# Graph-network layer in f32 on one core: the setup that builds the node table is reordered and its copies are shared between two engines

## What is computed

```python
h_s = s @ lin1_ws * a / 8                       # s: 64 scalars per node
h_v = einsum('nci,cd->ndi', v, lin1_wv) * a     # v: 32 vectors of 3
w   = silu(edge_scalars @ fc_w1) @ fc_w2        # 224 weights per edge
es, ev = h_s[edge_src], h_v[edge_src]           # gather of 160-float rows
# products of w, es, ev and edge_attr (e0, e1), summed over edge_dst
agg = segment_sum(products, edge_dst)
out = layernorm(x + gated(x @ sc + agg @ lin2))
```

## Time and profile before

| what | us |
| --- | --- |
| median of 3 runs, without profiler | 4014.98 |
| span of the profiled execution | 4805.3 |
| first gather of table rows begins (profiled) | 74.7 |
| last gather begins (profiled) | 4767.4 |

### The profile page before, as it was taken

How to read it: one execution, slowest core, us unless ns; L and a number is a source line. 1 busy time by engine, 2 the same in 40 slices (tenths; PEclk the granted TensorE clock), 3 DMA queues, 4 the chain that set the end, 5 groups by cost and what they waited for, 6 DMA issues and landing times.

```text
span 4805.3 us, 64016 instructions
## 1 busy us (share of the span) xinstructions
PE 3953.4 (82%) x18658; PEld 1603.5 (33%) x18658; DVE 2421.9 (50%) x7622; ACT 1987.8 (41%) x5178; POOL 2967.8 (62%) x3160
## 2 busy tenths in 40 slices
PE   8778888888888888888888888888888888888887
PEld 5233333333333333333333333333333333333333
DVE  5455545555454544555555445555545545454544
ACT  3344444444444444344444344444444434444444
POOL 3666666666666666666666666666666666666664
PEclk9999999999999999999999989999999999999999
DMA  6443434343434343334343334343434333333333
GB/s 216 146 106 102 106 102 106 102 107 102 108 99 108 102 106 97 105 102 106 103 107 101 104 99 105 102 106 103 107 103 106 102 105 103 105 103 104 103 103 87
DMA packets 366207, 515.47 MB, mean 107 GB/s; under 512 B 66498, under 2 KB 245578, under 8 KB 365486
## 3 DMA queue, kind: packets, MB, share of 16 engines
q0 software_dynamic: 150768, 256.60, 22.7%
q10 hardware_dynamic: 164378, 180.74, 12.1%
q1 hardware_dynamic: 50724, 74.13, 5.1%
HBM read 431.15 MB, written 80.06 MB: 106 GB/s over the span
## 4 chain that ended last, share of the span: by engine, by line
another core or an unknown queue 35%; ACT 21%; PE 20%; issue 14%; ACTq 8%; SPq 0%; DMA 0%; DVE 0%; DVEq 0%
ACT aggsb L759 13%; ACTq L778 6%; PE pst_e L1061 6%; PE psg L1074 5%; PE psg L1072 5%; ACT tsum L783 3%; PE psw L1053 3%; ACTq L766 2%; ACT L804 1%; ACT hid L749 1%; PE psx L1097 1%; PE psx L1045 1%; ACT vec_s L800 0%; ACT L749 0%
## 5 line engine op out<-in xcount | busy, mean ns | idle before, releaser
L710 POOL DMA_INDIRECT rows<-h_table,src_cols x3125 | 2953.5, 945 | 1799.9 <-issue 894.8
L557 DVE TENSOR_TENSOR prod<-psw,rows 128x384 f32<-128x384 f32 (+2 forms) x3128 | 1210.1, 449 | 1680.8 <-remote 1264.3
L1072 PE MATMUL psg<-tsum,shifts 128*64 128x320 f32 x3126 | 1101.8, 478 | 653.3 <-ACT tsum L783 462.6
L1053 PE MATMUL psw<-fc,hid 128*128 128x448 f32 x3128 | 1424.0, 579 | 7.7 <-issue 1.7
L759 ACT ACTIVATE aggsb<-psg 32x160 f32<-32x160 f32 x3128 | 917.0, 293 | 927.2 <-remote 744.2
L1074 PE MATMUL psg<-tsum,shifts 128*64 128x288 f32 x3126 | 1009.2, 449 | 0.0
L1053 PEld LDWEIGHTS psw<-fc,hid 128*128 128x128 f32 x3128 | 549.0, 196 | 949.6 <-issue 840.1
L1061 PE MATMUL pst_e<-prod,sel 128*32 128x448 f32 x6256 | 811.9, 593 | 2.4 <-issue 2.4
L1072 PEld LDWEIGHTS psg<-tsum,shifts 128*64 128x64 f32 x3126 | 385.9, 144 | 1122.2 <-ACT tsum L783 774.3
L783 ACT ACTIVATE tsum<-pst_e 128x448 f32<-128x448 f32 x782 | 424.8, 543 | 499.0 <-remote 369.4
L1045 PE MATMUL psx<-es,fc 128*128 128x512 f32 x782 | 415.7, 613 | 175.5 <-ACT turned L788 120.5
(11 more groups left out here) (151 smaller groups left out, 1511.2 us busy)
## 6 DMA issues: line engine op xcount, KB each, us to landing
es<-in_esP ACTq DMA_DIRECT2D x391, 256.0 KB
agg_table<-aggsb ACTq DMA_DIRECT2D x782, 80.0 KB
rows<-h_table,src_cols POOLq DMA_INDIRECT x3125
nag<-agg_table SPq DMA_DIRECT2D x96, 320.0 KB
nxin<-in_xN SPq DMA_DIRECT2D x96, 208.0 KB
h_table<-hrow ACTq DMA_DIRECT2D x24, 320.0 KB, 4.2
out<-yn SPq DMA_DIRECT2D x95, 80.0 KB
xa<-in_xaT SPq DMA_DIRECT2D x24, 256.0 KB, 4.0
```

The costliest lines, as they stand in the source:

```text
L557: return nc.vector.tensor_tensor(out, w_part, ev, ALU.mult)
L710: nc.gpsimd.indirect_dma_start(out=rows[:, u * QT + j, :], out_offset=None, in_=m.h, in_offset=bass.IndirectOffsetOnAxis(ap=m.src[:, t:t + ...
L1053: ins = nc.tensor.matmul(psw[b][:, 2 * c:2 * c + 2, 0:WN], hid[:, at:at + P], m.fc2[:].rearrange("p (t w) -> p t w", t=2)[:, :, 0:WN], sta ...
L1072: nc.tensor.matmul(psg[0:2 * W, 0:2 * AW].rearrange("p (s c) -> p s c", s=2), shifts[:, q % PRING, h, 0:2, :], low, start=(h == 0), stop=( ...
```

## The change

What it does, in the order of the work:

- SyncE loads chunks 0 to 3, then `m.dst` and `tbase`, then four new loads of `qbase` (each 32 partitions, a row of 782 int32 broadcast), and only then chunks 4 to 24. The loop over chunks is written out. The twelve `late` loads of fc1 and fc2 move from GpSimd's queue to the end of SyncE's. The load of the first 128 source columns moves from SyncE's end to the head of ScalarE's queue.
- Of each chunk ScalarE copies the first half (two groups, two instructions) and VectorE the second half (one `tensor_tensor` of 128x320). ScalarE issues the store of chunk n after its own copies of chunk n + 1.
- VectorE's other setup work is dealt out between its copies, unit by unit. Four pairs of 32-partition subtractions over `tbase` become two 128-partition ones with `qbase`; `after` is made from 780 columns in place of 3124 and its extreme is taken over these.
- `xa`, `xz` and `hrow` lie in the part of `m.e4` that is loaded later; `rows` and `prod` are allocated outside both blocks.
- SyncE waits for no store of the table. GpSimd waits for them at the head of the edge block, after its `value_load` and before its first gather; ScalarE waits for them before it loads the rest of `m.e4` in round 1.

TensorE's instructions per chunk stay the same.

```diff
         @block.sync
-            for c in range(1, SLOTS):
-                load_x(c, c, CB * P)
+            for c in range(1, 4):
+                load_x(c, CB * P)
             sp.dma_start(m.dst[:], io["dstT"]).then_inc(s_dst, 16)
             sp.dma_start(tbase[:], io["tile_base"].to_broadcast([P, TILES])).then_inc(s_dst, 16)
-            with sp.Fori(1, rounds) as i:
-                for c in range(SLOTS):
...
+            for j in range(QT):
+                sp.dma_start(qbase[W * j:W * j + W, :], io["quad_base"][j:j + 1, :].to_broadcast([W, QUADS])).then_inc(s_dst, 16)
+            for c in range(4, HCHUNKS):
+                load_x(c, CB * P)
+            load_x(HCHUNKS, rest)
             sp.dma_start(m.e4[:, 0:E4_FIRST, :], io["e4T"][:, 0:E4_FIRST, :]).then_inc(s_edge, 16)
-            sp.dma_start(m.src[:, 0:SRC_FIRST], io["srcT"][:, 0:SRC_FIRST]).then_inc(s_edge, 16)
-            for c in range(SLOTS):
-                sp.wait_ge(s_hout[c], 16 * (rounds + (2 if c == 0 else 0)))
-            sp.wait_ge(s_edge, 32)
+            sp.wait_ge(s_fc, 1)
+            sp.sem_inc(s_tick, 1)
+            for dst, src in late:
+                sp.dma_start(dst, src).then_inc(s_fcw, 16)
+            sp.wait_ge(s_edge, 16)
+            sp.wait_ge(s_fcw, n_fcw)
             sp.wait_ge(m.es_loaded, 16)
...
         @block.gpsimd
-            pool.wait_ge(s_fc, 1)
-            for dst, src in late:
-                pool.dma_start(dst, src).then_inc(s_w, 16)
-            pool.wait_ge(s_w, n_w)
+            pool.wait_ge(s_src, 16)
...
         @block.vector
+            def high_half(n, kind, c):
+                if kind == "h" and c >= SLOTS:
+                    dve.wait_ge(s_hout[c % SLOTS], 16 * (c // SLOTS))
+                    dve.sem_inc(s_tick, 1)
+                dve.wait_ge(s_high, second_halves(n) + 1)
+                out, scale = hrow[:, c % SLOTS, 2:CB, :], a_rows[:, CB * c + 2:CB * c + CB].unsqueeze(2)
+                nc.vector.tensor_tensor(out, psh[n % 2][:, 1, 0:2 * F].rearrange("p (b f) -> p b f", f=F),
+                                        scale.to_broadcast([P, 2, F]), ALU.mult).then_inc(s_highcp, 1)
...
+            for n, (kind, c) in enumerate(UNITS):
+                if n == 1:
+                    identity()
+                if n == 2:
+                    clear()
+                if n == 4:
+                    shift_pattern()
+                if n == 6:
+                    dve.wait_ge(s_dst, 32 + 16 * QT)
+                    then(local_nodes(0))
+                if n == 7:
+                    then(local_nodes(1))
+                if n == 8:
+                    window_starts()
+                if n == 9:
+                    window_steps()
+                if n == 10:
+                    reach()
+                if n == 11:
+                    extreme(0, m.local[:], ALU.max)
...
+                high_half(n, kind, c)
...
         @block.tensor
+            for n, (kind, c) in enumerate(UNITS):
                 keep_warm(256)
-                pe.wait_ge(s_xin[c], arrived)
+                pe.wait_ge(s_xin[c % SLOTS], 32 * (c // SLOTS + 1))
...
+                if n >= 2:
+                    pe.wait_ge(s_lowcp, n - 1)
...
+                    half(n, 0, [P, P], left, last).then_inc(s_low, 1)
+                    if n >= 2:
+                        pe.wait_ge(s_highcp, second_halves(n - 1))
+                    half(n, 1, [P, P], left, last).then_inc(s_high, 1)
...
         @block.scalar
+            act.dma_start(m.src[:, 0:SRC_FIRST], io["srcT"][:, 0:SRC_FIRST]).then_inc(s_src, 16)
...
+            for n, (kind, c) in enumerate(UNITS):
+                low_half(n, kind, c)
+                if n and UNITS[n - 1][0] == "h":
+                    store(UNITS[n - 1][1])
+            if UNITS[-1][0] == "h":
+                store(UNITS[-1][1])
...
 def edge_block(nc, io, m):
...
         @block.gpsimd
         def _(pool):
             miss = pool.value_load(m.misses[0:1, 0:1], min_val=0, max_val=CHECKS * P)
+            for c in range(len(m.h_stored)):
+                pool.wait_ge(m.h_stored[c], m.h_stores[c])
+                pool.sem_inc(stores_seen, 1)
```

More of the change, by code:

```diff
@@ L71, with unit_of, second_halves @@
 CHUNKED = NBLK // CB * CB
+HCHUNKS = NBLK // CB
+UNITS = [("h", c) for c in range(HCHUNKS + 1)]
+def unit_of(kind, c):
+    return UNITS.index((kind, c))
+def second_halves(n):
+    return sum(unit != ("h", HCHUNKS) for unit in UNITS[0:n])
 C_W = HID ** -0.5 * 16.0 ** -0.5
@@ L180, in setup_block @@
         s_xin = [sem(f"x_loaded{c}") for c in range(SLOTS)]
[L181 to L188, removed]
+        s_low = sem("low_half_in_psum")
+        s_high = sem("high_half_in_psum")
+        s_lowcp = sem("low_half_copied")
+        s_highcp = sem("high_half_copied")
+        s_tick = sem("setup_ticks")
+        s_hout = m.h_stored
+        rest = N - HCHUNKS * CB * P
+        done = CB * HCHUNKS
         block = ctx.enter_context(nc.Block())
@@ L317, in _ @@
[L317 to L331, removed]
@@ L339, in _, with self_weights, lin2_weights @@
-            then(nc.vector.tensor_reduce(ext[:, 6:7], after[:], AX.X, ALU.max))
+            def self_weights():
+                dve.wait_ge(s_w, n_w)
+                nc.vector.tensor_scalar(m.mscs[:], stage_sc[:], S ** -0.5, None, ALU.mult)
+                for i in range(3):
+                    r = slice(V * i, V * i + V)
+                    nc.vector.tensor_scalar(axis(m.mscv, r, i), scv[r, :], V ** -0.5, None, ALU.mult)
+            def lin2_weights(k):
+                for n, (part, to, scale) in enumerate(lin2_rows()):
+                    if n // 5 != k:
+                        continue
+                    r, chunk = slice(V * (n % 4), V * (n % 4) + V), m.w5[:, n // 4, :]
+                    if to is None:
+                        nc.vector.tensor_scalar(chunk[r, 0:SO], l2s[r, part, :], scale, None, ALU.mult)
+                    else:
+                        nc.vector.tensor_scalar(axis(chunk[:, SO:2 * SO], r, to), l2v[r, part, :], scale, None, ALU.mult)
@@ L392, in _, with half @@
-            for c in range(SLOTS):
-                chunk(c, 0, [P] * CB, 32, c >= 2)
-                if c == 0:
+            def half(n, v, widths, left, last):
+                for b in range(2):
+                    out = psh[n % 2][0:widths[b], v, F * b:F * b + P]
+                    nc.tensor.matmul(out, left[:, (2 * v + b) * P:(2 * v + b) * P + widths[b]], lw1[:], start=True, stop=True)
+                r = slice(S * v, S * v + S)
+                both = psh[n % 2][:, v, 0:2 * F].rearrange("p (b f) -> p b f", f=F)[:, :, P:F]
+                return nc.tensor.matmul(both, last[r, :], lw1z[r, :], start=True, stop=True)
@@ L427, in _ @@
-            for c in range(SLOTS):
-                chunk(c, 0, True)
-            with act.Fori(1, rounds) as i:
-                for c in range(SLOTS):
-                    chunk(c, i, False)
-            act.wait_ge(s_hout[0], 16 * rounds)
-            done = CB * chunks
-            for b, width in enumerate([P, LASTN]):
-                act.wait_ge(s_hps, done + 2)
-                nc.scalar.activation(hrow[0:width, 0, b, :], psh[0][0:width, 0, F * b:F * b + F], ACT.Copy,
-                                     scale=m.a[0:width, done + b:done + b + 1]).then_inc(s_hcp, 1)
```

257 lines of the change are left out of this document (148 added, 109 removed).

## The result

The changed kernel takes 4050.69 us (median of 4 runs, 4039.01 to 4064.72) against 4014.96 us; the ratio is 1.0090, with a 95% interval of 1.0062 to 1.0118. That is 36 us slower, where +7.8 us were forecast and the range ended at 4027.5. The four runs lie in two places: 4039.0 and 4040.0, and 4061.4 and 4064.7.

The account below looks back on a forecast made before the run. GpSimd's stream of gathers was taken to bound the kernel, so only the setup before the first gather counts: 5.8 (stall) + 2.6 (clock) - 0.6 (end) = +7.8 us, 4022.8 us; range 4016.5 to 4027.5.

Parts of the forecast that it names:

- Bound of the kernel: GpSimd issues one gather after another, 1.245 us each; only the first gather's start counts, us for us.
- the stops: GpSimd's waits beyond the usual gaps, 788 us, claimed to belong to the profiled execution only.
- The test in the prediction: Median less 74.7 us before the first gather and 37.9 at the end: 3902.4 us for 3124 intervals, 1.249 each.
- Copies by halves, checks, loops: Table setup: halved copies, fewer check passes and written out loops save 0; up to 0.8 us if VectorE is late once.
- VectorE's worst stretch: Chunks 8 to 11 of the table: 11.8 us of VectorE work against 9.8 of table, covered by some 3.9 us.
- Late loads and source columns: Setup loads on SyncE and ScalarE: 0; the twelve late loads up to 5.2 us without their cover.
- The stall: Chunk 4 lands behind dst and tbase, so TensorE stands from 19.7 to 25.5: +5.8 us (4.3 to 6.5).
- rival 1: No hold: chunk 4 lands in time beside the large loads; only -0.6 us counts, 4014.4 us; chance 0.13.
- The clock: TensorE's clock falls to 1.2 GHz in the idle time before chunk 4: +2.6 us (0 to 3.6).
- The end: End of setup: GpSimd reads its count and branches while stores land; first gather -0.6 us (0 to -1.0).
- rival 3: Table stores caught behind the source load after the barrier: up to 4.5 us more, about 4027.3 us; chance 0.12.
- rival 2: TensorE waits for chunk 4 but its clock does not fall: +5.8 - 0.6, 4020.2 us; chance 0.12.

Follow-up runs that it names:

- first profile of before: The kernel before, unchanged, in its first profiled execution: span 4805.3 us, against an unprofiled median of 4014.98 us.
- interleaved kernel: Changed kernel with loads ordered chunks 0 to 7, dst, chunk 8, tbase, chunks 9 and 10, qbase, rest; VectorE's dependent pieces later: 4016.86 us.
- second profile of before: The kernel before, unchanged, profiled once more: 4014.57 us, span 4012.8 us.
- ten runs of one kernel: Interleaved kernel with all copies on ScalarE and 128 in place of 256 columns in the matmul ahead of each chunk: 4031.53 us.
- the kernel with the filled wait: Changed kernel with six 512 column matmuls issued before the wait for chunk 4: 4024.23 us.
- the one with the short opening: Interleaved kernel with all copies on ScalarE and four in place of six 512 column matmuls in the opening: 4014.98 us.

## Why the prediction was wrong

**Bound of the kernel: right.** From the first gather to the last are 3904.9 to 3907.8 us in every traced kernel (the first profile of before, with its stops, left out), and behind it 31.6 to 35.3; the stops belonged to that one profiled execution. The test in the prediction took 37.9 us for the end from the execution with the stops, and so 3902.4 for the gathers; without stops it is 31.7 and 3905.8. "After the first gather nothing changes" held to 2.5 us of the 25.4.

**Copies by halves, checks, loops: 0, right for the setup, wrong for the kernel.** One second half took 0.49 us where 0.45 was taken; TensorE waited for no copy in the interleaved kernel. The sum for VectorE's worst stretch is added up wrongly: its terms give 13.4 us, not 11.8, so it would fall behind by 3.6 us and not 2.0, still less than the cover of 3.9. But the halves cost some 3 us behind the last gather (last section), where the prediction had nothing change. Late loads and source columns: 0, right; the interleaved kernel has both and starts its gathers at 74.22.

**The stall: right in place and cause.** +5.8 forecast (4.3 to 6.5), 5.1 measured. Two errors offset each other in the size, which is luck: tbase landed at 20.2, 2.3 us ahead of the 22.5 of the sum, and chunk 4's second tile, the last, came 4.6 us behind it, at 24.8, where 3.0 were taken. The rule of the Trainium skill that was weighed there ("DMA: Bandwidth & Descriptors", section on queues, rings and completion order, that completion is not FIFO per issuing engine) did not decide: this trace shows chunk 4 behind the large loads, as chunk 8 was in the earlier trace rows. The descriptors' ring order, of which the same section speaks, agrees: chunk 4 came 4.6 us behind tbase. It spoke against rival 1 from the start, more than the rule on completion spoke for it.

**The clock: the term that was mis-sized.** "I take +2.6 us, the opening's, where TensorE was continuously fed as it is here." It measured 18.7 us in the profiled run, one of the faster pair. (The prediction's own row gives 2.5, and 3.6 was its upper end.) The fall was right and so was the level. What failed was the length of the slow stretch: 42 us and not the 5.0 of the opening or the 7.2 of the edge block. Both rows that it was taken from show TensorE coming back on wide matmuls: 512 columns in the opening, 512 and 448 in the edge block. The work behind the stall is another: matmuls of 128 and 64 columns between weight loads, with one of 256 per chunk. "Fed" was read from the busy column, and by that column the two are alike. The run with six 512 column matmuls behind the wait shows the difference, 3 us until the clock is back against 42; the one with them ahead of the wait shows that without the fall only the wait is left. A second error was small and went the other way: at half clock a chunk took 4.39 us, 1.8 times 2.44, not twice.

The Trainium skill, "TensorE: Matmul & The Clock Gate", Part 1, says that the clock is set by how busy TensorE has been recently. The changed kernel's trace agrees for the fall, 3.0 us into the idle time; for the rise it does not if busy is read from the profile, where TensorE stood at 40.00 of 40.00 us with the clock at 0.50.

**The end: right in sum, in part by luck.** -0.6 forecast, 5.1 - 4.6 = 0.5 measured. The forecast has ScalarE free 2.5 us behind TensorE's last product and the first gather 2.1 us later; measured are 1.8 (until 95.38) and 2.8, with 0.7 for the eight waits where 0.4 was taken. No store was caught behind the source load (rival 3): the chain leaves the waits as fast as GpSimd can run them. Rival 1 fell with chunk 4's landing, rival 2 with the clock.

**The range** took the clock's term between 0 and 3.6 us, both from rows whose work was not that of the table. No row of before had a stretch of the table itself at half clock, and the range should have said so: the upper end had to be the whole of the table behind the stall at 1.2 GHz. With the 1.95 us by which a chunk turned out longer that is 20.5 x 1.95 = 40 us, and the traced run of the kernel before with dst and tbase first came near it: first gather at 117.62, some 37 us more than its wait of 5.2.

## What to carry over

A late load costs what it delays and, where it drops TensorE's clock, a share of all that TensorE does until the clock is back; price that with the work that follows, not with the opening's. Where the stage behind is made of short matmuls, fill an unavoidable wait with wide ones, or put them right behind it: in the traced runs the first cut the loss at the first gather from 23.5 to 5.9 us and the second to 13.0, and either way the runs agreed within 5 us. Count the bytes ahead of each load in SyncE's order before a large one is moved forward, and prefer dealing the large ones out; here even 391 KB were too much.

## What was not expected of the hardware

- One program, two times: 4009.6 to 4010.0 and 4031.2 to 4035.1 us in ten runs of one kernel. An idle time of 1.1 us preceded the fall of the clock in the traced run, and the fall came only 1.6 us after TensorE had taken up work again; after one of 1.5 us in the kernel with the filled wait, and one of 0.7 us in the one with the short opening, it stayed. What decides at such lengths was not settled.
- Copies by halves in the setup go with a later end of the kernel. From the last gather to the end are 32.7 to 35.3 us in all seven traced kernels that have them, and 31.6 to 31.8 in all six traces without them (the second profile of before among these). The interleaved kernel and the one with all copies on ScalarE differ in the copies alone: 35.1 us (3979.3 to 4014.4) against 31.6, with first gathers 0.4 us apart and medians 3.3 us apart. Part of it can be the clock: the interleaved kernel has a dip right behind its last gather, here in windows of 3 us:

```profile
3976.30:3979.30 3.00, 0.61 (x4) 0.39 (x4) 2.57 (x9) 0.00 (x0) 2.09 (x4) 0.97 0.90 302
3979.30:3982.30 3.00, 3.00 (x15) 1.25 (x17) 0.74 (x2) 0.63 (x2) 0.90 (x1) 0.50 0.51 166
3982.30:3985.30 3.00, 3.00 (x15) 1.06 (x13) 2.77 (x10) 1.87 (x6) 0.00 (x0) 0.96 0.02 4
```

  It cannot be all: the kernel with SyncE's waits put back also takes 35.1 us behind its last gather, and the changed kernel 33.4, both with the clock at 1.00 there. How copies in the setup reach the end of the kernel was not tried and stays open.
- Of the 25.4 us by which the changed kernel's profiled run is longer than the second profile of the kernel before, 2.5 are not in the first gather: its stream of gathers is 3906.6 us and its end 33.4, against 3905.8 and 31.7. The end is the pattern of the point above; for the stream no cause was tried.
